# Cross-attention and FFN layer on one core: FFN input tiles transposed by VectorE through DRAM, first weight blocks prepared beside the output projection

## The chip, the cores and the metric

The kernel runs on one core of one Trainium2 chip. The metric is the device time of one execution, in microseconds; lower is better. The runs before the change took 2531.85, 2536.68 and 2537.15 us (median 2536.68).

## The reference

One transformer layer for 16 sequences of 112 tokens (1792 tokens) of width 1024, with a context of 375 vectors for each sequence, all in float32:

```
x = x + attention(layernorm(x), ctx, ctx) @ Wo      # 32 heads, 8 key/value heads
n = layernorm(x)
g = n @ (w1 * w1_scale).T ; u = n @ (w3 * w3_scale).T   # 1024 -> 3584, a scale for each 128x128 block
x = x + (silu(g) * u) @ (w2 * w2_scale).T               # 3584 -> 1024
```

The second layernorm has no weights; its result `n` is the FFN's input. The matrix products want it transposed, with the 1024 features on the partitions.

## The kernel before, in words

The program has four stages, one after the other: `queries`, `attention`, `mixing` (L933), which is the output projection with the residual and the second layernorm, and `ffn` (L1115). Each of the last two is one block of five instruction streams (TensorE, VectorE, ScalarE, GpSimd, and SyncE for the transfers); the streams run in the written order and meet by semaphores. A stage's block ends when all its streams have ended, SyncE's with waits for its last stores. Every product of float32 operands is done as three products of a high and a low part (`split_product`, L84 to L86), so operands are first copied to the high part by ScalarE and the rest is taken by VectorE (`to_lo`, L90).

`mixing` goes over 14 tiles of 128 tokens. For tile t, SyncE loads the attention's output and the rows of x (`load_tile`), ScalarE and VectorE split the attention's output (L1000, L90), TensorE makes two column halves of 512 in two PSUM banks with 48 matmuls, and VectorE runs `residual_norm(t)`: two residual adds (L1042) with the statistics of each half (L1047), the aggregate, GpSimd's power for 1/sqrt (L992), and the normalization (L1058) into `xn`. TensorE then transposes the eight 128x128 blocks of `xn` of the tile before (`transposes(t - 1)`, L1099) after the products of tile t, and ScalarE copies them (`out_x`, L1012) into `xT` for the first seven tiles, or into `xs`, which SyncE stores to `x_scratch`, for the last seven. SyncE also stores the sum to `y_scratch` (L978). In SyncE's order, `load_tile(t + 1)` stands behind the wait for the adds of tile t - 1, in front of the wait for those of tile t.

`ffn` works with Strassen-like sums: a product of a pair of 2x2 blocks is done by seven matmul groups instead of eight. There are 28 first-layer weight blocks (`mi`), w1 and w3 in turn, in two passes over the two halves of the tokens. A weight block is loaded raw (`load_raw`, L168, four transfers of 32 partitions each, by which the quarters of the columns land on the quarters of the partitions), scaled by ScalarE (L1540), transposed by VectorE in blocks of 32x32 (`make_wT`, L1643; with that placement this is the full transpose), summed (`sums`, L1666 to L1671) and split (L1558, L90). The seven inputs `x_source(g, i)` are blocks of `xT` and sums of them (`x_sums`, L1694), split in the same way (L1567, L90). Before its loop the stage has a head: weight block 0, the x sums, all seven splits of x and of weight block 0, and the transposes of weight block 1. TensorE takes product i of block mi when both splits of index i are there; its product i = 5 of block 0 waits also for the first add of results (`add`, L1699), which stands in VectorE's stream behind the head. What comes later (second pass, down projection) is as in the code and is touched by the change in small places only.

Of the kernel before, what the change touches and what calls it, by code (L numbers as in the profile page):

```python
# [21 lines left out]
def build_program(nc, x, ctx, wq, wk, wv, wo, w1, w1_scale, w3, w3_scale, w2, w2_scale, out):  # L22
# [49 lines left out]
    y_scr = nc.dram_tensor("y_scratch", [TOK, D], f32).ap()  # L72
    h_scr = nc.dram_tensor("h_scratch", [7, P, NP, HALF], f32).ap()
# [23 lines left out]
    with top:  # L97
# [34 lines left out]
        raw_loaded = sem("raw_loaded")  # L132
        q_stored = [sem(f"q_stored{c}") for c in range(NG * J)]
# [799 lines left out]
        def mixing(xT):  # L933
            with ExitStack() as st:
# [9 lines left out]
                yb, xn = sb("yb", [P, 2, D]), sb("xn", [P, 2, KT, P])  # L944
                xs = sb("xs", [P, 2, KT, P])
# [7 lines left out]
                t_done, t_out = s_("t_done"), s_("t_out")  # L953
                o_bank, t_bank = bank[0:2], bank[2:4]

                with nc.Block() as block:
                    @block.sync
                    def _(sp):
# [8 lines left out]
                        def store_xT(t):  # L967
                            sp.wait_ge(t_out, 2 * t + 2)
                            cols = slice((t - MT) * P, (t - MT + 1) * P)
                            sp.dma_start(x_scr[:, :, cols], xs[:, t % 2, :, :]  # L970
                                         ).then_inc(xT_stored[t % 2], 16)
# [10 lines left out]
                        store_xT(NT_TOK - 1)  # L982

                        for s in range(2):
                            sp.wait_ge(res_stored[s], 16 * NT_TOK // 2)
                            sp.wait_ge(xT_stored[s], 16 * ((MT + s) // 2))
# [9 lines left out]
                    def _(act):  # L996
# [6 lines left out]
                        def out_x(t):  # L1003

                            if t >= MT:
                                wait(act, xT_stored[t % 2], 16 * ((t - MT) // 2))
                            for kh in range(2):
                                act.wait_ge(t_done, 2 * t + kh + 1)
                                ks = slice(KH * kh, KH * kh + KH)
                                dst = (xT[:, ks, t * P:(t + 1) * P] if t < MT  # L1010
                                       else xs[:, t % 2, ks, :])
                                nc.scalar.activation(dst, t_bank[kh][:, :].rearrange(  # L1012
                                    "p (k q) -> p k q", k=KH), ACT.Copy).then_inc(t_out, 1)
# [6 lines left out]
                        for t in range(1, NT_TOK):  # L1020
                            if t + 1 < NT_TOK:
                                split_attention(t + 1)
                            out_x(t - 1)
                            if t == 4:
                                place_scales(act)
                        out_x(NT_TOK - 1)

                    @block.vector
                    def _(dve):
# [5 lines left out]
                        def residual_norm(t):  # L1035
# [3 lines left out]
                            for n in range(2):  # L1039
                                cols = slice(n * FB, (n + 1) * FB)  # L1040
                                dve.wait_ge(o_done, 2 * t + n + 1)
                                nc.vector.tensor_tensor(yb[:, slot, cols], o_bank[n][:, :],  # L1042
# [13 lines left out]
                            wait(dve, t_done, 2 * (t - 1))  # L1056

                            nc.vector.tensor_scalar(  # L1058
                                xn[:, slot, :, :].rearrange("p b (q j) -> p q b j", q=Q4),
                                yb[:, slot, :].rearrange("p (q b j) -> p q b j", q=Q4, j=BL),  # L1060
                                aggr[:, 0:1], rstd[:], ALU.subtract, ALU.mult
# [53 lines left out]
        def ffn(xT):  # L1115
            with ExitStack() as st:
# [275 lines left out]
                with nc.Block() as block:  # L1392
# [140 lines left out]
                    def _(act):  # L1533
# [63 lines left out]
                        for mi in range(2 * NM):  # L1597
                            P_, nxt = mi // 2, mi + 1 < 2 * NM
                            for i in range(7):
# [11 lines left out]
                                if nxt:  # L1611
                                    split_w(mi + 1, i)
# [220 lines left out]
```

## Time and profile before

| | before |
|---|---|
| runs, us | 2531.85, 2536.68, 2537.15 |
| the profiled execution's own time, us | 2538.41 |
| its span, first to last instruction, us | 2536.6 |
| mean granted TensorE clock | 0.977 of full speed |
| TensorE matmuls busy | 2427.8 us, 96% |
| VectorE busy | 1698.4 us, 67% |
| ScalarE busy | 979.2 us, 39% |
| `mixing`, first split to the last x_scratch store | about 862 to 1041 us |
| `ffn`, from its first ScalarE instruction | 1041.17 us on |

Rows of a timeline give the start in us from the span's start, the duration, the engine (SPq is SyncE's transfer queue; its duration is that of issuing), the line, what is written and read with the size, and in brackets how long the engine was idle before it and what ended that. A busy share is no measure of what a stage's end depends on; the chain of waits and the timeline of the stage are.

### The profile page before, as it was taken

Reading aid. Unit: us, or ns where it says so; the run is one execution under the profiler, and the core shown is the slowest. Engines: PE = TensorE matmul, PEld = TensorE weight load, DVE = VectorE, ACT = ScalarE, POOL = GpSimd, SP = SyncE. Lnnn points to the kernel's source line nnn. Section 1 sums busy time; section 2 is a strip of 40 time slices with the busy share of each in tenths; the row PEclk is TensorE's granted clock in tenths of the full one; section 3 lists DMA queues with packets and bytes.
Section 4 is the critical chain, followed back from the end, with each engine's and each line's share of the span. In section 5 each row is a group of like instructions: output and inputs, shape, how many; then the busy total and the mean of one; then the engine's idle time right before and its main releaser. Section 6 shows DMA issues by size and latency. Waiting matters only on the chain.

```text
span 2536.6 us, 35412 instructions
## 1 busy us (share of the span) xinstructions
PE 2427.8 (96%) x12682; PEld 2071.4 (82%) x12682; DVE 1698.4 (67%) x2639; ACT 979.2 (39%) x1673; POOL 559.2 (22%) x305
## 2 busy tenths in 40 slices
PE   7998999999999799599999998999999999999999
PEld 6997878878875488489999987988988978888887
DVE  6425777777776344688888888888888874445442
ACT  3212445445444321354444444444433443233231
POOL 1000344454455300001111111322333320000000
PEclk9998999999998799799999999999999999999999
DMA  7535555555545335456555564565776687555652
GB/s 226 173 92 138 140 139 139 144 134 142 143 110 131 95 127 170 119 183 184 159 176 156 158 179 134 158 174 190 208 209 176 172 287 234 172 174 160 183 161 86
DMA packets 369146, 408.04 MB, mean 161 GB/s; under 512 B 125824, under 2 KB 324096, under 8 KB 359152
## 3 DMA queue, kind: packets, MB, share of 16 engines
q1 hardware_dynamic: 369008, 406.22, 56.1%
q8 instruction: 85, 1.39, 0.2%
q14 instruction: 53, 0.43, 0.1%
HBM read 252.99 MB, written 152.70 MB: 160 GB/s over the span
## 4 chain that ended last, share of the span: by engine, by line
PE 44%; DVE 8%; DMA 3%; issue 2%; SPq 1%; ACT 1%; DVEq 0%; ACTq 0%
PE bank L84 15%; PE bank L85 14%; PE bank L86 14%; DMA stash<-weight_scratch 3%; DVE g_WL L90 2%; DVE g_XL L90 1%; DVE g_su L1699 1%; DVE xT L1655 1%; SPq L1431 1%; DVE stash L1667 1%; DVE stash L1666 1%; DVE stash L1669 1%; ACT stash L1548 0%; ACT g_WH L1558 0%; DVE stash L1643 0%
## 5 line engine op out<-in xcount | busy, mean ns | idle before, releaser
L84 PE MATMUL bank<-g_XH,g_WH 128*128 128x448 f32 (+1 forms) x2254 | 848.0, 376 | 51.8 <-DVE g_su L1699 24.2
L85 PE MATMUL bank<-g_XL,g_WH 128*128 128x448 f32 (+1 forms) x2254 | 845.0, 375 | 0.0
L86 PE MATMUL bank<-g_XH,g_WL 128*128 128x448 f32 (+1 forms) x2254 | 844.8, 375 | 0.0
L84 PEld LDWEIGHTS bank<-g_XH,g_WH 128*128 128x128 f32 x2254 | 425.2, 189 | 115.8 <-DVE g_WL L90 52.8
L86 PEld LDWEIGHTS bank<-g_XH,g_WL 128*128 128x128 f32 x2254 | 425.2, 189 | 54.1
L85 PEld LDWEIGHTS bank<-g_XL,g_WH 128*128 128x128 f32 x2254 | 425.4, 189 | 53.5
L1558 ACT ACTIVATE g_WH<-stash 128x512 fp32r<-128x512 f32 x392 | 241.7, 627 | 427.6 <-PE bank L86 247.0
L90 DVE TENSOR_TENSOR g_WL<-stash,g_WH 128x512 fp32r<-128x512 f32 (+1 forms) x417 | 336.0, 809 | 77.4 <-ACT g_WH L1558 49.4
L696 DVE TENSOR_REDUCE a_nm<-bank 112x1 f32<-112x375 f32 x512 | 264.9, 531 | 116.9 <-PE bank L831 113.3
L800 ACT ACTIVATE a_pr<-bank 125x448 f32<-125x448 f32 x384 | 204.8, 545 | 208.2 <-PE bank L907 153.7
L649 POOL TENSOR_TENSOR a_prsum<-a_pr 125x1792 f32<-125x1792 f32 x32 | 129.3, 4039 | 365.3 <-ACT a_pr L800 365.3
L1699 DVE TENSOR_TENSOR g_su<-bank,g_su 128x448 f32<-128x448 f32 x280 | 170.8, 610 | 35.6 <-PE bank L86 35.3
L831 PE MATMUL bank<-a_kst,a_qst 96*112 96x376 f32 x512 | 183.2, 367 | 5.8 <-DVE a_nm L696 2.6
L907 PE MATMUL bank<-a_qst,a_kst 98*125 98x448 f32 x384 | 148.3, 391 | 2.8 <-ACT a_pr L800 2.4
L831 PEld LDWEIGHTS bank<-a_kst,a_qst 96*112 96x112 f32 x512 | 91.7, 179 | 69.7 <-DVE a_nm L696 32.6
L1498 POOL TENSOR_TENSOR g_Sh<-stash 128x448 f32<-128x448 f32 x28 | 32.6, 1165 | 492.5 <-DVE stash L1704 492.5
L645 POOL TENSOR_TENSOR a_prsum<-a_prsum,a_pr 125x1792 f32<-125x1792 f32 x32 | 128.7, 4022 | 1.8
L678 DVE RECIPROCAL a_l<-a_l 128x112 f32<-128x112 f32 x128 | 106.6, 839 | 25.8 <-ACT a_l L754 25.8
L84 PE MATMUL bank<-a_w_h,a_cT_h 128*125 128x256 f32 x384 | 111.8, 291 | 0.0
L86 PE MATMUL bank<-a_w_h,a_cT_l 128*125 128x256 f32 x384 | 107.8, 281 | 0.0
L85 PE MATMUL bank<-a_w_l,a_cT_h 128*125 128x256 f32 x384 | 107.7, 280 | 0.0
L1285 ACT ACTIVATE g_WH<-stash 128x1792 fp32r<-128x1792 f32 x25 | 42.6, 1703 | 156.8 <-PE bank L86 146.3
(132 smaller groups left out, 3592.8 us busy)
## 6 DMA issues: line engine op xcount, KB each, us to landing
stash<-in_L_ffn_w SPq DMA_DIRECT2D x168, 256.0 KB, 5.1
weight_scratch<-stash SPq DMA_DIRECT2D x28, 1024.0 KB, 7.7
stash<-weight_scratch SPq DMA_DIRECT2D x28, 1024.0 KB, 7.4
h_scratch<-g_Sh SPq DMA_DIRECT2D x112, 224.0 KB, 3.9
down_scratch<-xT SPq DMA_DIRECT2D x98, 256.0 KB, 3.1
stash<-in_ctx SPq DMA_DIRECT2D x48, 500.0 KB
stash<-h_scratch SPq DMA_DIRECT2D x25, 896.0 KB, 6.7
a_qst<-q_scratch SPq DMA_DIRECT2D x96, 224.0 KB, 4.7
```

Of the source, the lines that this page charges most:

```text
L84: pe.matmul(acc, lh, rh, start=first, stop=False, skip_group_check=onto)
L85: pe.matmul(acc, lh, rl, start=False, stop=False, skip_group_check=onto)
L86: return pe.matmul(acc, ll, rh, start=False, stop=last, skip_group_check=onto)
L90: return nc.vector.tensor_tensor(dst, src, hi.bitcast(f32), ALU.subtract)
L645: pool.tensor_tensor(prsum[:], prsum[:], pr[0:CK, :, 2, :], ALU.add).then_inc(all_added, 1)
L649: pool.tensor_tensor(prsum[:], pr[0:CK, :, 0, :], pr[0:CK, :, 1, :], ALU.add).then_inc(two_added, 1)
L696: nc.vector.tensor_reduce(nm[:, 1 - par, h:h + 1], s_bank[h % 2][0:SQ, 0:SK], AX.X, ALU.max, negate=True).then_inc(max_done, 1)
L800: nc.scalar.activation(pr[0:CK, r, c, :], st_bank[u % 2][0:CK, 0:J * SQ], ACT.Exp, scale=SCALE).then_inc(exp_done, 1)
L831: pe.matmul(s_bank[h % 2][0:SQ, 0:SKP], qst[0:96, 1 - par, g, j * SQ:(j + 1) * SQ], kst[0:96, 1 - par, g, :], start=True, stop=True).then_ ...
L907: pe.matmul(st_bank[u % 2][0:CK, 0:J * SQ], kst[0:98, par, g * R + r, c * CK:(c + 1) * CK], qst[0:98, par, g * R + r, :], start=True, stop ...
L1558: nc.scalar.activation(WH[:, i, :, :], w_source(mi, i), ACT.Copy).then_inc(w_hi, 1)
L1699: nc.vector.tensor_tensor(su[:, slot, :], acc[mi % 2][:, 0:TB], su[:, other, :], ALU.add).then_inc(summed, 1)
```

## The change

The transposes of the layernorm's output leave TensorE. `residual_norm(t)` writes `xn` in plain order, SyncE stores it to a new DRAM tensor `n_scr`, waits until that store has landed, and loads it back with four transfers in the same quarter placement as the raw weights (`load_turn`); VectorE transposes it with two 32x32-block transposes (`turn_tile`, called by `turn`). For the last tile this is done in `ffn`, while block 0 runs. The matmuls of a tile now use one of two pairs of banks, by the tile's parity. SyncE's order in a tile is new, and so is VectorE's, where `turn(t - 1)` stands in front of `residual_norm(t)`. Part of the head of `ffn` (weight block 0 whole, weight block 1 up to its sums, two of the x sums) is spread over tiles 6 to 12 of `mixing` by the class `Ahead`. The semaphores of the down projection's `load_y` are shared by two tiles, with a wait for the tile two before.

```diff
+        def load_turn(sp, dst, t, loaded):
+            cols = n_scr[t * P:(t + 1) * P, :].rearrange("(c i) (q n) -> q i c n", i=BL, q=Q4)
+            for q in range(Q4):
+                sp.dma_start(dst[q * BL:(q + 1) * BL, :, :], cols[q]).then_inc(loaded, 16)
+
+        def turn_tile(src, dst, turned):
+            src = src.rearrange("p c (b j) -> p b c j", j=BL)
+            dst = dst.rearrange("p b (c j) -> p b c j", j=BL)
+            nc.vector.transpose(dst[:, 0:KH], src[:, 0:KH])
+            return nc.vector.transpose(dst[:, KH:KT], src[:, KH:KT]).then_inc(turned, 1)
...
+                        def load_xr(t):
+                            sp.wait_ge(xn_stored[t % 2], 16 * (t // 2 + 1))
+                            wait(sp, turned, t - 1)
+                            load_turn(sp, xr[:, t % 2, :, :], t, xr_loaded[t % 2])
+
                         for t in range(NT_TOK):
-                            if 1 <= t < NT_TOK - 1:
-
-                                sp.wait_ge(y_done, 2 * t)
-                                load_tile(sp, t + 1)
                             sp.wait_ge(y_done, 2 * t + 2)
+                            if t + 2 < NT_TOK:
+                                load_tile(sp, t + 2)
                             sp.dma_start(y_scr[t * P:(t + 1) * P, :], yb[:, t % 2, :]
                                          ).then_inc(res_stored[t % 2], 16)
                             if t > MT:
                                 store_xT(t - 1)
-                        store_xT(NT_TOK - 1)
+                            sp.wait_ge(xn_done, t + 1)
+                            sp.dma_start(n_scr[t * P:(t + 1) * P, :], xn[:, t % 2, :]
+                                         ).then_inc(xn_stored[t % 2], 16)
+                            if t + 1 < NT_TOK:
+                                load_xr(t)
+                            if t == 9:
+                                ahead.load_raw(sp)
...
+                        def turn(t):
+                            dve.wait_ge(xr_loaded[t % 2], 64 * (t // 2 + 1))
+                            if t >= MT:
+                                wait(dve, xT_stored[(t - 1) % 2], 16 * ((t - MT + 1) // 2))
+                            turn_tile(xr[:, t % 2, :, :], xT[:, :, t * P:(t + 1) * P] if t < MT
+                                      else xs[:, :, :], turned)
...
                         for t in range(1, NT_TOK):
                             if t + 1 < NT_TOK:
                                 split_attention(t + 1)
+                            turn(t - 1)
                             residual_norm(t)
+                            ahead.vector(t, turned, w_lo)
...
                         for t in range(1, NT_TOK):
                             products(t)
-                            transposes(t - 1)
-                        transposes(NT_TOK - 1)
...
+                    def scalar(t):
+                        if t == 6:
+                            act_scale_raw(0, 0)
+                            act_scale_raw(0, 1)
+                        for i in W_AT.get(t, ()):
+                            act_split_w(0, i)
+                        if t == 11:
+                            act_scale_raw(1, 0)
+                            act_scale_raw(1, 1)
...
+                    def vector(t, turned, wo_split):
+                        if t == 7:
+                            nc.vector.wait_ge(wo_split, NG * J)
+                            nc.vector.wait_ge(sc_placed, 3 * Q4)
+                            for n in range(4):
+                                dve_make_wT(0, n)
+                        if t == 8:
+                            dve_sums(0)
+                        if t == 9:
+                            nc.vector.wait_ge(turned, MT)
+                            dve_x_sums(0, 0)
+                            dve_x_sums(0, 1)
+                        for i in W_AT.get(t, ()):
+                            dve_split_w(0, i)
+                        if t == 12:
+                            for n in range(4):
+                                dve_make_wT(1, n)
+                            dve_sums(1)
+
+                W_AT = {9: (0, 1), 10: (2, 3), 11: (4, 5), 12: (6,)}
...
                         split_x(0, 0)
-                        split_w(0, 0)
-                        x_sums(0, 1)
-                        x_sums(0, 2)
+                        dve_x_sums(0, 2)
                         split_x(0, 1)
-                        split_w(0, 1)
                         split_x(0, 2)
-                        split_w(0, 2)
-                        x_sums(0, 3)
-                        for n in range(4):
-                            make_wT(1, n)
+                        dve_x_sums(0, 3)
                         for i in range(3, 7):
                             split_x(0, i)
-                            split_w(0, i)
...
+                                if mi == 0 and i == 1:
+                                    dve.wait_ge(last_loaded, 64)
+                                    turn_tile(last_in, last_out, last_turned)
...
                         for mi in range(2 * NM):
                             if mi == 2:
+                                sp.wait_ge(last_turned, 1)
+                                sp.dma_start(x_scr[:, :, HALF - P:HALF], last_out
+                                             ).then_inc(last_stored, 16)
...
                 def load_y(sp, r, t):
+                    if t >= 2:
+                        sp.wait_ge(d_y_loaded[r][t % 2], y_count(r, t - 2))
```

## Rows read from the trace of the kernel before

**Rows 1.** The page: busy shares, and the chain that ended last.

```profile
PE 2427.8 (96%) x12682; PEld 2071.4 (82%) x12682; DVE 1698.4 (67%) x2639; ACT 979.2 (39%) x1673; POOL 559.2 (22%) x305
...
PE 44%; DVE 8%; DMA 3%; issue 2%; SPq 1%; ACT 1%; DVEq 0%; ACTq 0%
```

**Rows 2.** Timeline of TensorE in `mixing`: a tile's products begin, its transposes follow.

```profile
1008.91 0.48 PE L84 MATMUL bank<-m_w_h,m_a_h 128*128 128x512 f32 x1
...
1019.90 1.04 PE L1099 MATMUL bank<-ident,m_xn 128*128 128x128 f32 x8
```

**Rows 3.** Timeline of VectorE: second residual adds of tiles 0, 1, 12 and 13.

```profile
879.85 0.67 DVE L1042 TENSOR_TENSOR m_yb<-bank,stash 128x512 f32<-128x512 f32 x1
...
889.55 0.68 DVE L1042 TENSOR_TENSOR m_yb<-bank,stash 128x512 f32<-128x512 f32 x1
...
890.88 0.67 DVE L1042 TENSOR_TENSOR m_yb<-bank,stash 128x512 f32<-128x512 f32 x1
...
1020.10 0.69 DVE L1042 TENSOR_TENSOR m_yb<-bank,stash 128x512 f32<-128x512 f32 x1 [0.34 <-PE bank L86]
...
1022.62 0.81 DVE L1058 TENSOR_SCALAR m_xn<-m_yb,m_aggr,m_rstd 128x1024 f32<-128x1024 f32 x1 [0.66 <-POOL m_rstd L992]
...
1031.88 0.69 DVE L1042 TENSOR_TENSOR m_yb<-bank,stash 128x512 f32<-128x512 f32 x1 [3.93 <-PE bank L86]
```

**Rows 4.** Timeline of SyncE's queue: transfers that follow tile 2's adds.

```profile
903.02 0.33 SPq L978 DMA_DIRECT2D y_scratch<-m_yb  x1
903.39 0.55 SPq L157 DMA_DIRECT2D stash<-attn_scratch  x1
903.99 0.92 SPq L159 DMA_DIRECT2D stash<-in_x  x1
```

**Rows 5.** Windows (stretch, length, engines, clock, DMA share, GB/s): those three transfers.

```profile
903.50:904.00 0.50, 0.50 (x4) 0.42 (x3) 0.43 (x3) 0.33 (x1) 0.00 (x0) 1.00 0.32 131
904.00:908.50 4.50, 4.50 (x22) 3.72 (x21) 0.97 (x2) 0.28 (x1) 0.55 (x1) 1.00 1.00 325
908.50:909.00 0.50, 0.50 (x4) 0.42 (x3) 0.00 (x0) 0.50 (x1) 0.00 (x0) 1.00 0.24 90
```

**Rows 6.** Windows: the same with an x_scratch store between; that store alone.

```profile
1009.50:1010.00 0.50, 0.50 (x4) 0.42 (x3) 0.45 (x3) 0.41 (x1) 0.00 (x0) 1.00 0.30 123
...
1016.50:1017.00 0.50, 0.50 (x4) 0.42 (x3) 0.00 (x0) 0.50 (x1) 0.00 (x0) 1.00 0.07 25
...
1033.50:1036.50 3.00, 1.09 (x8) 0.86 (x8) 1.02 (x3) 0.47 (x1) 0.55 (x1) 1.00 0.92 319
...
1038.50:1040.00 1.50, 0.00 (x0) 0.00 (x0) 0.00 (x0) 0.00 (x0) 0.00 (x0) 0.50 0.98 290
1040.00:1040.50 0.50, 0.00 (x0) 0.00 (x0) 0.00 (x0) 0.00 (x0) 0.00 (x0) 0.50 0.31 87
```

**Rows 7.** One line of the DMA issues: count, size, median us to landing.

```profile
y_scratch<-m_yb SPq DMA_DIRECT2D x14, 512.0 KB, 3.1
```

**Rows 8.** Window during one raw weight block's load (four transfers of 32 partitions).

```profile
1047.50:1051.00 3.50, 0.00 (x0) 0.00 (x0) 3.50 (x3) 0.00 (x0) 0.00 (x0) 0.50 1.09 198
```

**Rows 9.** Timeline of VectorE and ScalarE: first instructions of `ffn`.

```profile
1041.17 2.56 ACT L1540 ACTIVATE stash<-stash,sc 128x512 f32<-128x512 f32 x4 [4.06 <-PEq L956]
...
1042.54 2.53 DVE L1643 STREAM_TRANSPOSE stash<-stash 128x512 f32<-128x512 f32 x4 [7.32 <-ACT stash L1540]
```

**Rows 10.** Timeline of the head: a split of x, a sum, the first results' add.

```profile
1056.10 1.70 ACT L1567 ACTIVATE g_XH<-stash 128x1792 fp32r<-128x1792 f32 x1 [10.27 <-DVE stash L1694]
...
1057.83 2.03 DVE L90 TENSOR_TENSOR g_XL<-stash,g_XH 128x1792 fp32r<-128x1792 f32 x1 [1.76 <-ACT g_XH L1567]
1059.77 0.68 DVE L90 TENSOR_TENSOR g_WL<-stash,g_WH 128x512 fp32r<-128x512 f32 x1
...
1080.13 0.69 DVE L90 TENSOR_TENSOR g_WL<-stash,g_WH 128x512 fp32r<-128x512 f32 x1
...
1081.49 0.71 PE L84 MATMUL bank<-g_XH,g_WH 128*128 128x448 f32 x1 [6.36 <-DVE g_su L1699]
```

More of the change, by code:

```diff
@@ L930, in _, with mixing @@
                         sums(B - 1, 1)
-        def mixing(xT):
+        def mixing(xT, ahead):
             with ExitStack() as st:
@@ L1092, in products @@
                                 last.then_inc(o_done, 1)
-                        def transposes(t):
-                            pe.wait_ge(xn_done, t + 1)
-                            for kh in range(2):
-                                wait(pe, t_out, 2 * t + kh - 1)
-                                for k in range(KH):
-                                    last = pe.transpose(t_bank[kh][:, k * P:(k + 1) * P],
-                                                        xn[:, t % 2, KH * kh + k, :], ident[:])
-                                last.then_inc(t_done, 1)
                         pe.wait_ge(a_lo, 1)
@@ L1178, in hcols, with act_scale_raw @@
                     return slice(g * TB, (g + 1) * TB)
+                def act_scale_raw(mi, s):
+                    p, m = mi // 2, mi % 2
+                    nc.scalar.wait_ge(raw_loaded, 64 * (mi + 1))
+                    for a in range(2):
+                        part = raw[:, 4 * a:4 * a + 4, s * P:(s + 1) * P]
+                        nc.scalar.activation(part, part, ACT.Copy,
+                                             scale=sc13[:, m, 2 * p + a, s:s + 1]
+                                             ).then_inc(raw_scaled, 1)
@@ new lines, in dve_sums @@
+                def dve_sums(mi):
+                    a11, a12, a21, a22 = [quarter(mi, a, b) for a in range(2) for b in range(2)]
+                    s1, s2, s3, s4 = (S[:, k, :, :] for k in range(4))
+                    if mi < NM:
+                        nc.vector.wait_ge(wT_made, 4 * mi + 4)
+                    else:
+                        nc.vector.wait_ge(wT_loaded[mi % 2], 16 * ((mi - NM) // 2 + 1))
+                    wait(nc.vector, w_lo, 7 * mi)
+                    nc.vector.tensor_tensor(s1, a21, a22, ALU.add).then_inc(S_made, 1)
+                    nc.vector.tensor_tensor(s3, a11, a21, ALU.subtract).then_inc(S_made, 1)
+                    nc.vector.wait_ge(S_made, 4 * mi + 1)
+                    nc.vector.tensor_tensor(s2, s1, a11, ALU.subtract).then_inc(S_made, 1)
+                    nc.vector.wait_ge(S_made, 4 * mi + 3)
+                    nc.vector.tensor_tensor(s4, a12, s2, ALU.subtract).then_inc(S_made, 1)
@@ new lines, in dve_split_w, with dve_x_sums @@
+                def dve_split_w(mi, i):
+                    nc.vector.wait_ge(w_hi, 7 * mi + i + 1)
+                    to_lo(WL[:, i, :, :], w_source(mi, i), WH[:, i, :, :]).then_inc(w_lo, 1)
+                def dve_x_sums(g, n):
+                    b11, b12, b21, b22 = (block_of(s, t) for s in range(2) for t in range(2))
+                    out, left, right = ((t1[:, :, :], b12, b11), (b12, b22, b12),
+                                        (t2(g), b22, t1[:, :, :]), (t2(g), b21, t2(g)))[n]
+                    if n in (1, 2, 3):
+                        nc.vector.wait_ge(T_made, 4 * g + {1: 1, 2: 1, 3: 3}[n])
+                    if g:
+                        nc.vector.wait_ge(x_loaded_, 16)
+                        if n == 2:
+                            nc.vector.wait_ge(wT_made, 4 * NM)
+                    if n == 3:
+                        nc.vector.wait_ge(x_lo, 7 * g + 2)
+                    nc.vector.tensor_tensor(out, left, right, ALU.subtract
+                                            ).then_inc(T_made, 1)
@@ L1245, in load_a, with y_count @@
                                  ).then_inc(d_a_loaded[n % 2], 16)
+                def y_count(r, t):
+                    return sum(32 * len(rows(r, u)) for u in range(t % 2, t + 1, 2))
                 def load_y(sp, r, t):
+                    if t >= 2:
+                        sp.wait_ge(d_y_loaded[r][t % 2], y_count(r, t - 2))
                     for at, n, tok in rows(r, t):
@@ L1728, in _ @@
                                 dve.wait_ge(prod, 7 * mi + i + 1)
-                                if i == 0 and nxt:
-                                    sums(mi + 1)
+                                if i == 0 and nxt and mi:
+                                    dve_sums(mi + 1)
                                 if i == 1:
```

190 lines of the change are left out of this document (72 added, 118 removed).

## The prediction

> **What bounds the kernel now.** I read the page first: TensorE is busy 96% of the span, and the chain that ended last is TensorE's in its largest part [rows 1]. Then the timelines of the stretch that the change touches, engine by engine. In `mixing` the reader is to see a stage paced by TensorE: tile 13's products begin at 1008.91 and its transposes are 1.04 us behind them; VectorE's second residual add waits for matmuls (0.34 and 3.93 us idle before it) [rows 2, 3]. I call the end of that add Y. Y of tile 0 is 879.85 + 0.67 = 880.52, Y of tile 13 is 1032.57: 152.05 us for 13 tiles, 11.70 each [rows 3]. The head of `ffn` is the other thing: its first instruction runs at 1041.17, and product i = 5 of block 0 starts only at 1081.49, after 6.36 us of waiting for VectorE [rows 9, 10]. There VectorE is the bound. So I count three pieces: Y0 to Y13, Y13 to the start of `ffn` (1041.17 - 1032.57 = 8.60), and from there to that product (40.32).
>
> **Tiles of mixing.** Removed: eight transposes per tile on TensorE (1.04) [rows 2] and the copies by ScalarE. By TensorE alone a tile would then take at most 1019.90 - 1008.91 = 11.0 us. But VectorE's new order makes a ring: xn(t), store to DRAM, its landing, load back, its landing, turn(t), and only then the adds of tile t + 1, from which xn(t + 1) comes. Nothing in it overlaps with itself, so its length is the least period of a tile. Step by step from Y(t), for tiles before the first x_scratch store:
>
> SyncE issues at once the attention load, the x load and the y store; they are the three transfers of [rows 4] in another order. Their bytes began 0.8 us after the first issue (903.02 to 903.84, by the share 0.32 of that half microsecond) and ended at 908.62: 4.8 us of transfer [rows 5]. The normalization ends 1022.62 + 0.81 - 1020.79 = 2.64 after Y [rows 3], so the new store is issued at Y + 2.66, while the three are still moving until Y + 0.03 + 0.8 + 4.8 = 5.65. With one more store in between, the busy stretch grew from 4.8 to 6.7 us (1009.85 to 1016.53) at a full share [rows 5, 6]: transfers of this queue add up. I therefore put the new store behind them. It has the shape of the y store: y and x_scratch stores together run at 319 GB/s, 3.3 us for 1.05 MB, the x_scratch store alone at 290 GB/s, 1.8 to 1.9 us, so 1.4 for it [rows 6]. It ends at 7.05. The y store lands 3.1 us after issue [rows 7], of which 0.8 and 1.4 are explained, so completion is 0.9: landed at 7.95. The load back: 0.8, then 0.52 MB in quarters of 32 partitions, which go at 198 GB/s (2.65 us) [rows 8], then 0.9: 4.35, landed at 12.3. The turn: two of the transposes of which four took 2.53, so 1.27 [rows 9]. The adds with everything ready: 889.55 to 891.55, 2.0 [rows 3]. The next Y is at Y + 15.6.
>
> From t = 8 to 11 the x_scratch store (1.9) is ahead of the new one too: 17.5. At t = 12 there is no tile to load: y, x_scratch and new store end at 0.03 + 0.8 + 1.4 + 1.9 + 1.4 = 5.55, and the ring is 5.55 + 0.9 + 4.35 + 3.27 = 14.1. Sum: 8 x 15.6 + 4 x 17.5 + 14.1 = 208.9 us against 152.05: +56.9.
>
> Bounds of the period. Below, if the new store overtakes the queue: 2.66 + 3.1 + 4.35 + 3.27 = 13.4, or 13 x 13.4 = 174 us (+22). Above, if one more transfer's length shows in every ring, because the quarter loads start late or the halves of the queue are not as well filled as now: 1.9 more per tile [rows 6], +82. I take the sum, because the shares of [rows 5, 6] stand at 1.00 while the transfers add up.
>
> The Trainium skill's page "DMA: Bandwidth & Descriptors", section "Anatomy of one DMA", gives about 2.0 us plus bytes over 436 GB/s, for the GpSimd path; 3.2 for the new store, where [rows 7] have 3.1. By it without a queue the period is the lower bound. The same page of the Trainium skill, "Queues, rings and completion order", says that descriptors on each engine are consumed in ring order, which by the lengthening in [rows 6] the trace agrees with; by that the period is the 15.6 to 17.5. The Trainium skill's rule there ("Rules for kernel authors") that a DMA which reads what another wrote must wait for the other's completion speaks against this change: the completion is paid twice in the ring.
>
> **What lies beside the ring.** TensorE has two pairs of banks now: tile t + 2's products wait for Y(t) and for its splits, and are needed only at Y(t + 1) + 13.6; at half clock too (a warm-up would cost some 2 us) they have over 10 us to spare, so TensorE's saved transposes and lower clock cost or give nothing. The work of `Ahead` on VectorE stands between xn(t) at Y + 2.64 and the turn at Y + 12.3; 9.7 us, of which the attention split needs an estimated 1.4 (twice a 512-wide split of 0.68) [rows 10]. The longest are t = 9, two x sums of 2.03 and two splits of 0.68, 5.4 us, and t = 12, 2.53 for transposes, four sums and a split of 0.7, 6.0 us [rows 9, 10]. Hidden, so 0. If the ring's waits were gone, tile 12 would need 6.0 + 1.4 + 1.27 + 2.0 + 2.64 = 13.3 us of VectorE against TensorE's 11.0, and lose 2. The added raw load at t = 9 (1.05 MB at 198 GB/s, 5.3 us) lies behind the load back and delays the next tile by under 1 us. I leave it at 0.
>
> **End of the stage.** After Y13 the new store's bytes end at 5.55, as at t = 12. Before, `ffn` began 1.0 us after the last store's bytes (about 1040.15 to 1041.17) [rows 6, 9]. So 6.55 instead of 8.60: -2.05.
>
> **Head of ffn.** Left on VectorE's path: the high split of x by ScalarE and its handover (1056.10 to 1057.83, 1.73), and then at VectorE split 0, x sum 2; x sum 2 has to end before ScalarE makes the high part of split 1, a second 1.73 plus 0.05; splits 1 and 2, x sum 3, splits 3 to 6. That is two handovers and nine operations at a pitch of 1.94 (1057.83 to 1059.77): 3.5 + 17.5 = 21.0. Then split, add and product start as before (1080.13 to 1081.49, 1.36): 22.35 [rows 10]. Against 40.32: -18.0. The turn of tile 13 stands behind that add; its 1.27 meets product i = 5 in progress, 2.5 to 4.5 us long, so 0, at most 1.3 lost. TensorE's clock may be up at that point instead of down, up to 2 us gained; I take 0.
>
> **Later parts.** SyncE's new x_scratch store at mi = 2 and the wait for it, some 3 to 4 us, stand where its raw loads have waited for VectorE; `load_y` waits for loads issued two tiles before. 0, at most 4.
>
> **The sum.** 2538.4 (the profiled execution) + 56.9 - 2.05 - 18.0 = 2575.2. That execution is 1.7 above the median of the runs, so 2573.5; I say 2574, slower by 1.5%.
>
> **The rivals.** *The ring without a queue*: the new store passes the loads. +22 - 20 = +2, 2539: no change, in which the ring's cost eats the head's gain. For it: the store is issued only 2.6 us behind. Against it: [rows 6]. The point that decides is a period of 11.70 + 20.05/13 = 13.24 us. *TensorE still paces the tiles*: the round trip from xn(t) to the turn ends within what TensorE's 11.0 leaves, 11.0 - 2.64 - 3.27 = 5.1 us. Then 13 x (11.0 - 11.70) = -9.1, and with -20.05 it is 2508, faster. For it: nothing but that transfers could overlap more than now; against it: one landing alone is 3.1 [rows 7] and there are two. *A longer ring*: the four quarter loads begin late or collide with the next tile's loads, 1.9 more per tile, +25: 2599. That the change does not remove the transposes or move the blocks can be excluded from the code.
>
> **Chances.** Forecast 0.73, longer ring 0.09, no queue 0.11, TensorE paces 0.07. The range of 8 in 10 is 2542 to 2602: it holds the forecast with steps of the ring off by 2 us per tile, the longer ring, and leaves out the faster case and most of the unchanged. A difference of 0.2% (5 us) is about what a measurement of this kernel can tell from none. Faster 0.11 (TensorE paces, and the shorter half of the unqueued ring), same 0.05, slower 0.84.
>
> **What would show it.** In the profile after: the second residual adds 15 to 18 us apart, longer from tile 8 on; VectorE idle for many us before the turn's transposes, released by the load from `norm_scratch`; TensorE idle some 5 us in each tile of `mixing`; `ffn` begins about 6.5 us after the last add, and product i = 5 some 22 us after that. The prediction is wrong if the adds are 11 us apart, if TensorE's products release them, or if the new store lands some 3 us after its issue.

## The result, and the profile after

The changed kernel takes 2586.6 us (median of 4 runs, 2583.8 to 2592.9), the kernel before 2536.4 beside it: 1.0206 times as long, 95% interval 1.0189 to 1.0223. Forecast was 2574, 1.5% slower.

The spans of the two profiled executions (2536.6 and 2582.9) part into the pieces of the prediction. Y is again the end of a tile's second residual add. The last piece starts at product i = 5 of block 0 of `ffn`.

| piece, us | before | after | change | predicted |
|---|---|---|---|---|
| up to Y0 | 880.5 | 878.0 | -2.6 | 0 |
| Y0 to Y13 | 152.05 | 220.3 | +68.2 | +56.9 |
| Y13 to the start of `ffn` | 8.60 | 6.5 | -2.1 | -2.05 |
| from there to product i = 5 | 40.32 | 22.36 | -18.0 | -18.0 |
| from there to the end | 1455.1 | 1455.8 | +0.6 | 0 |
| span | 2536.6 | 2582.9 | +46.3 | +36.8 |

The page of the kernel after, its busy shares and the chain that ended last, against [rows 1]:

```profile
PE 2431.6 (94%) x12570; PEld 2072.0 (80%) x12570; DVE 1711.8 (66%) x2667; ACT 966.0 (37%) x1645; POOL 557.8 (22%) x305
...
PE 44%; DVE 5%; DMA 2%; issue 1%; SPq 1%; ACT 0%; POOL 0%; DVEq 0%
```

TensorE is about as busy as before (2431.6 and 2427.8 us) in a longer span, so the added time is idle time. Its 112 transposes are gone, but its granted clock over the tiles fell from 1.00 to 0.86, and its products took longer. The chain of this kernel reaches back only to 1195.66 us, behind the tiles and the head of `ffn`, so its shares say nothing of either. The waits of the kernel after, 875 to 1100 us (total, times, longest), say who waits in `mixing`:

```profile
PE bank L85 <- DVE m_a_l L91: 45.1, 11, 7.3
DVE xT L182 <- DMA m_xr<-norm_scratch: 43.9, 7, 6.6
DVE m_xs L182 <- DMA m_xr<-norm_scratch: 39.8, 6, 9.1
```

VectorE stands 83.7 us, once in each of 13 tiles, for the load back. That it is idle before 12 of the 13 turns for 5.9 to 9.1 us is the ring seen from VectorE (before the last, 2.1). TensorE's 45 us are a consequence: the attention tile of tile t + 2 is loaded only once the adds of tile t are done, and its split follows. From Y0 on VectorE's adds never waited for TensorE (the one such wait, 4.41 us, is at tile 0). One turn of the ring, tile 2 to tile 3, on VectorE (the add that is Y2; the turn of tile 2; the two adds of tile 3), against [rows 3]:

```profile
911.02 0.68 DVE L1055 TENSOR_TENSOR m_yb<-bank,stash 128x512 f32<-128x512 f32 x1
...
924.83 0.71 DVE L182 STREAM_TRANSPOSE xT<-m_xr 128x512 f32<-128x512 f32 x1 [6.28 <-DMA m_xr<-norm_scratch]
...
926.06 0.65 DVE L1055 TENSOR_TENSOR m_yb<-bank,stash 128x512 f32<-128x512 f32 x1
...
927.36 0.67 DVE L1055 TENSOR_TENSOR m_yb<-bank,stash 128x512 f32<-128x512 f32 x1
```

On SyncE's queue, against [rows 4]:

```profile
911.73 0.55 SPq L159 DMA_DIRECT2D stash<-attn_scratch  x1
912.32 0.66 SPq L161 DMA_DIRECT2D stash<-in_x  x1
913.02 0.43 SPq L996 DMA_DIRECT2D y_scratch<-m_yb  x1
914.37 0.32 SPq L1001 DMA_DIRECT2D norm_scratch<-m_xn  x1
920.39 0.80 SPq L176 DMA_DIRECT2D m_xr<-norm_scratch  x2
```

And in windows (stretch, length, the engines, clock, DMA share, GB/s), against [rows 5]:

```profile
911.50:913.00 1.50, 1.50 (x8) 1.24 (x7) 1.25 (x6) 0.00 (x0) 0.05 (x1) 1.00 0.00 0
913.00:913.50 0.50, 0.50 (x4) 0.41 (x3) 0.00 (x0) 0.00 (x0) 0.50 (x1) 1.00 0.47 131
913.50:914.50 1.00, 1.00 (x6) 0.72 (x4) 0.81 (x1) 0.00 (x0) 0.00 (x0) 1.00 0.83 232
914.50:919.50 5.00, 1.16 (x6) 0.75 (x5) 1.22 (x1) 1.06 (x1) 0.00 (x0) 1.00 0.97 346
919.50:920.00 0.50, 0.50 (x3) 0.42 (x2) 0.00 (x0) 0.00 (x0) 0.00 (x0) 0.66 0.35 139
920.00:920.50 0.50, 0.50 (x3) 0.34 (x2) 0.00 (x0) 0.00 (x0) 0.00 (x0) 0.50 0.00 0
```

The reader is to see the ring in these three views. Y2 is 911.70. The new store is issued at Y + 2.67, and four transfers fill the queue until about 919.7. Only then does SyncE get the landing and issue the load back (920.39), and the turn starts at 924.83; Y3 is 928.03, a period of 16.33 us. The DMA issues of the kernel after (count, size, median us to landing) give the same in one line each; [rows 7] had 3.1 for the first:

```profile
y_scratch<-m_yb SPq DMA_DIRECT2D x14, 512.0 KB, 6.3
norm_scratch<-m_xn SPq DMA_DIRECT2D x14, 512.0 KB, 6.2
m_xr<-norm_scratch SPq DMA_DIRECT2D x52, 128.0 KB, 3.0
```

The last piece looks unchanged (+0.6), yet has a hole. The kernel after, timelines of SyncE, ScalarE and TensorE in the first weight blocks of `ffn`:

```profile
1155.82 0.52 SPq L1580 DMA_DIRECT2D x_scratch<-g_Sh  x1
1165.79 0.35 SPq L1586 DMA_DIRECT2D xT<-x_scratch  x1
...
1171.76 6.80 SPq L170 DMA_DIRECT2D stash<-in_L_ffn_w  x4
```
```profile
1187.40 1.34 ACT L1196 ACTIVATE stash<-stash,sc 128x512 f32<-128x512 f32 x2 [9.67 <-DMA stash<-in_L_ffn_w]
```
```profile
1202.92 0.71 PE L85 MATMUL bank<-g_XH,g_WH 128*128 128x448 f32 x1 [6.48 <-DVE g_su L1755]
```

SyncE stores the last x block, stands 10 us for its landing, and issues the next raw weights only at 1171.76, behind eight other transfers issued since 1165.79 (it takes 6.80 us to issue the four, 1.79 at 1136.50). ScalarE waits for them, then VectorE, then TensorE for 6.48 us. What hides this loss in the piece's sum is told under the eighth and tenth experiment.

### The profile page after: what moved, and what is told of

Same layout as the page of the kernel before. It is cut to its first block, busy times and chain, and to the rows that moved or that the text cites. A ratio compares the mean times of both kernels' runs of the same rounds, so it can differ in the third digit from the quotient of the medians.

```text
span 2582.9 us, 35260 instructions
## 1 busy us (share of the span) xinstructions
PE 2431.6 (94%) x12570; PEld 2072.0 (80%) x12570; DVE 1711.8 (66%) x2667; ACT 966.0 (37%) x1645; POOL 557.8 (22%) x305
## 3 DMA queue, kind: packets, MB, share of 16 engines
q1 hardware_dynamic: 379088, 420.90, 56.9%
## 4 chain that ended last, share of the span: by engine, by line
PE 44%; DVE 5%; DMA 2%; issue 1%; SPq 1%; ACT 0%; POOL 0%; DVEq 0%
PE bank L85 15%; PE bank L87 15%; PE bank L86 15%; DMA stash<-weight_scratch 2%; DVE g_WL L91 1%; DVE g_su L1755 1%; DVE g_XL L91 1%; DVE xT L1747 1%; DVE stash L1234 1%; SPq L1559 0%; DVE stash L1233 0%; DVE stash L1236 0%; DVE stash L1760 0%; ACT stash L1671 0%; ACT g_WH L1206 0%
## 5 line engine op out<-in xcount | busy, mean ns | idle before, releaser
L85 PE MATMUL bank<-m_w_h,m_a_h 128*128 128x512 f32 x224 | 98.1, 438 | 54.4 <-DVE m_a_l L91 45.1
```

The lines of the kernel that those rows point to most:

```text
L85: pe.matmul(acc, lh, rh, start=first, stop=False, skip_group_check=onto)
```

## The experiments

Theory: the ring decides, because the turn stands ahead of the next tile's adds, and its length is the queue plus two landings. Rivals: the added traffic alone is the cost (15 MB through one queue); VectorE's added work; TensorE's granted clock (0.86 over 880 to 1098 us). Each kernel is the changed one with the edit shown; ratios are to the kernel before, run beside it (its medians there were 2529.9 to 2532.6).

**1. The turn behind the next normalization.**

```
 for t in range(1, NT_TOK):          # VectorE
-    turn(t - 1)
     residual_norm(t)
     ahead.vector(t, turned, w_lo)
+    turn(t - 1)
```
(and SyncE issues `store_xT(t - 1)` behind the new store)

> VectorE runs the turn of tile t - 1 behind the adds and the normalization of tile t instead of ahead of them (the x_scratch store follows it in SyncE's order); every transfer, wait for a landing and operation is kept. Ring theory (the adds of tile t + 1 wait for store, landing, load, landing, turn of tile t): the ring is cut, tiles up to 7 go at TensorE's 11 us, those after at the 12 to 12.5 us that SyncE's waits need; first to last second add 8 x 11.2 + 5 x 12.5 = 152 us instead of 220; total 2586.6 - 68 + 2 = about 2520. Rival, the transfers' own load or VectorE's added work paces the stage: no change by the order, 2575 to 2590.

Measured: 2523.8 us, 0.9967 (0.9952 to 0.9982), so about 60 us less than the changed kernel with every byte and instruction of it kept. Y0 to Y13 is 153.5, as expected. On VectorE the second add of tile 3 (Y3), its normalization, the turn of tile 2, and the add that is Y4:

```profile
913.84 0.67 DVE L1055 TENSOR_TENSOR m_yb<-bank,stash 128x512 f32<-128x512 f32 x1
...
916.34 0.81 DVE L1070 TENSOR_SCALAR m_xn<-m_yb,m_aggr,m_rstd 128x1024 f32<-128x1024 f32 x1 [0.66 <-POOL m_rstd L1017]
918.61 0.71 DVE L182 STREAM_TRANSPOSE xT<-m_xr 128x512 f32<-128x512 f32 x1 [1.46 <-DMA m_xr<-norm_scratch]
...
924.69 0.67 DVE L1055 TENSOR_TENSOR m_yb<-bank,stash 128x512 f32<-128x512 f32 x1
```

The period is 10.85 us with the same turn in it, and the wait for the load back has shrunk to 1.46. Its waits, 875 to 1050 us:

```profile
DVE xT L182 <- DMA m_xr<-norm_scratch: 11.0, 6, 3.9
...
PE bank L85 <- DVE m_a_l L91: 8.3, 5, 5.3
```

The ring theory holds: the position of the turn costs what was measured, and neither VectorE's work nor the traffic does. The granted clock over the tiles is 0.98 here, so this run doesn't test the clock by itself; in the changed kernel no add waited for TensorE from Y0 on, and the clock is off the path for that reason. One period is still long, 16.4 from Y10 to Y11, two tiles behind the raw load; in experiment 9, where that load is issued two tiles earlier, the long one (15.4) is from Y8 to Y9.

**2. The same traffic, without the wait for it.** The turn reads `xn` in place.

```
 def turn(t):
-    dve.wait_ge(xr_loaded[t % 2], 64 * (t // 2 + 1))
+    dve.wait_ge(xn_done, t + 1)
...
-    turn_tile(xr[:, t % 2, :, :], ...
+    turn_tile(xn[:, t % 2, :].rearrange("p (c n) -> p c n", n=DQ), ...
```

> The turn reads the normalized tile in place, without the way through DRAM, so the quarters of the columns are not exchanged between partitions and the FFN gets wrongly placed inputs; the store to DRAM and the load back are still issued and waited for by SyncE, at their places, but VectorE does not wait for them. Ring theory: only the wait cost time; adds 11 us apart up to tile 8, at most 12.5 behind; about 2516. Rival, the traffic of 1 MB more per tile costs it by contention: more than half of the 50 us stays, 2560 or more.

Measured: 2528.0 us, 0.9984 (0.9973 to 0.9994); Y0 to Y13 162.1. So of the 68 us some 10 are left (152.05 to 162.1), nearly all of it in the periods from t = 8 to 11 (13.9, 14.0, 16.8, 13.5 us): there SyncE issues the new store at 1003.65, say, and the load back behind its landing at 1014.05, and all later loads stand behind that wait. These 10 are the traffic and SyncE's own wait together, and the traffic's part is small: the first experiment has the same bytes and needs 153.5. The other 58 are VectorE's wait.

**3. The y and x_scratch stores behind the load back.**

```
+    load_xr(t)                       # SyncE, order within a tile
     sp.dma_start(y_scr[...], yb[...])
     if t > MT: store_xT(t - 1)
-    load_xr(t)
```

> The ring is kept, but the y store and the x_scratch store are issued behind the load back instead of ahead of the new store. Queue theory (transfers of the queue go one after the other): landing of the new store comes 1.5 us earlier up to tile 8 and 3 us earlier at tiles 8 to 11, 8 x 1.5 + 4 x 3 = 24 us less, about 2563. Rival, the ring is made of fixed latencies and the queue ahead does not matter: no change, 2587.

Measured: 2580.7 us, 1.0193 (1.0172 to 1.0214): a miss, 2563 was expected. From tile 1 up to tile 8 the step is there: 14.5 to 15.8 us per tile instead of 16.3 to 16.8, 1.5 less on the mean as expected, with the load back issued at Y + 6.8 to 7.3 (tile 0 keeps 16.85). From tile 8 on the periods are 17 to 18, because of a wait I had left out. VectorE in this kernel:

```profile
1014.72 0.71 DVE L182 STREAM_TRANSPOSE m_xs<-m_xr 128x512 f32<-128x512 f32 x1 [8.29 <-DMA x_scratch<-m_xs]
```

The turn now waits for the store of the single `m_xs` buffer, which had been sent to the end of the queue. In all Y0 to Y13 gained 12.7 us; the end of the stage lost 2.6 and the last piece 6.7 (below). The y store ahead of the new store is a part of the ring, 1.5 us of it per tile; from tile 8 on, moving it and the x_scratch store only moves the wait.

**4. The moved blocks alone.** Transposes by TensorE and copies by ScalarE as before, no trip through DRAM; two bank pairs and `Ahead` as in the changed kernel.

```
-    turn(t - 1)                      # VectorE
+    transposes(t - 1)                # TensorE, into bank[4:6]
+    out_x(t - 1)                     # ScalarE
```

> One part of the change alone: the first weight blocks and two x sums spread over the tiles, the banks in pairs, but the transposes by TensorE with ScalarE's copies as before, nothing through DRAM. The head part is worth -18 us by my sum and the tiles stay at 11.7 us, so about 2518 (2536.4 - 18). Rival, the work moved into the tiles delays VectorE's adds or collides with the attention split: tiles longer, 2530 or more.

Measured: 2517.3 us, 0.9944 (0.9926 to 0.9963). Y0 to Y13 is 151.5 with a pitch of 11.78, TensorE's, and the head 22.37. The blocks prepared ahead cost these tiles nothing, and they are the gain of the change at the head of `ffn`; only the 2.1 us at the end of the stage are not theirs.

**5. The load back issued a tile later.** Over the first experiment, SyncE issues `load_xr(t - 1)` at the head of tile t.

```
     for t in range(NT_TOK):          # SyncE
+        if 0 < t < NT_TOK - 1:
+            load_xr(t - 1)
         sp.wait_ge(y_done, 2 * t + 2)
...
-        if t + 1 < NT_TOK: load_xr(t)
+        if t == NT_TOK - 2: load_xr(t)
```

> As in the run with the turn behind the normalization, but SyncE never waits for the new store's landing: it issues the load back of tile t - 1 at the head of tile t, when that store has long landed, and VectorE turns tile t - 1 behind the normalization of tile t; for tile 12 alone the order of the changed kernel is kept. Ring theory with the sum of transfers as the next bound: tiles before 8 at TensorE's 10.9 us, those from 8 on at the 11.7 us of their six transfers; first to last add 147 us; 6 us below the first cut, tail 6.5 instead of 10.3: about 10 us faster than that run. Rival, the transfers collide (load back ahead of the attention load delays the splits that TensorE waits for): no faster than it.

Measured: 2531.9 us, 0.9999 (0.9984 to 1.0015): a miss, 10 us less than the first was expected. Y0 to Y13 is 162.4, 9 us more than the first. The other tiles gain nothing (Y0 to Y12 143.5, there 142.1), as the rival had it, and most of the loss is one tile: Y12 to Y13 takes 18.94 (11.41 there), because there the turn stands ahead of the adds again, as in the changed kernel. VectorE before Y13:

```profile
1033.45 0.70 DVE L182 STREAM_TRANSPOSE m_xs<-m_xr 128x512 f32<-128x512 f32 x1
...
1040.97 0.71 DVE L182 STREAM_TRANSPOSE m_xs<-m_xr 128x512 f32<-128x512 f32 x1 [6.22 <-DMA m_xr<-norm_scratch]
```

**6. The turn through DRAM alone,** with no block prepared during `mixing`.

```
 def vector(t, turned, w_lo):         # and scalar(t), load_raw(sp)
-    if t == 7: ... dve_make_wT(0, n)
-    if t == 8: dve_sums(0)
...
+    pass
```

> The other part of the change alone: the transposes go through DRAM and VectorE as in the changed kernel, but nothing of the FFN's head is moved into the tiles. The ring sets the tiles with or without that work, so the head comes back in full, +18 us, and the tiles keep their 16 to 19 us (220 us from first to last add, some 3 less without the raw load at tile 9): the changed kernel + 15 to 18. Rival, the moved work lengthens the ring: the tiles get clearly shorter without it and less than 10 us are lost.

Measured: 2610.1 us, 1.0304 (1.0277 to 1.0332), by the ratios 25 more than the changed kernel, where 15 to 18 were expected. Its Y0 to Y13 is 218.4, 2 less than with the moved blocks; the tenth experiment, the changed kernel again, has 223.5, so executions of one kernel differ by more than that. TensorE's product i = 5:

```profile
1145.03 0.71 PE L85 MATMUL bank<-g_XH,g_WH 128*128 128x448 f32 x1 [6.35 <-DVE g_su L1742]
```

That is 40.3 us after the start of `ffn`: the 18 of the head are back in full. The other 7 are in the last piece (1462.8 for 1455.8).

**7. One landing instead of two.** The load back reads as many bytes from the input x and waits for no store.

```
-    sp.wait_ge(xn_stored[t % 2], 16 * (t // 2 + 1))
-    load_turn(sp, xr[...], t, xr_loaded[t % 2])
+    load_turn(sp, xr[...], t, xr_loaded[t % 2], x.rearrange("b q n -> (b q) n"))
```

> The load back takes the same amount in the same four quarters from the kernel's input x instead of the normalized tile, and is issued right behind the new store without waiting for its landing; so the FFN gets untreated inputs. The ring loses the gap between the store's last byte and the first byte loaded, 1.3 us at tile 2, and keeps both transfers: from 16.4 to about 14.9 up to tile 8 and 16.6 behind it, first to last add about 200 instead of 220, the changed kernel - 20. Rival, one landing is worth a whole latency of 3 us: 13.4 per tile, - 40.

Measured: 2563.1 us, 1.0115 (1.0087 to 1.0142). SyncE and VectorE in tile 3:

```profile
911.65 0.33 SPq L1001 DMA_DIRECT2D norm_scratch<-m_xn  x1
912.02 1.04 SPq L176 DMA_DIRECT2D m_xr<-in_x  x1
```
```profile
920.21 0.71 DVE L182 STREAM_TRANSPOSE xT<-m_xr 128x512 f32<-128x512 f32 x1 [4.11 <-DMA m_xr<-in_x]
```

The load back is issued at once, and still lands only at the end of the queue: the periods are 14.3 to 14.6 (t = 1 to 7), 2.1 less than after, where the forecast of the ring gives 1.7 less (0.8 and 0.9); from t = 8 to 11, 15.8 to 16.4. Y0 to Y13 is 193.2 where about 200 were expected; that the time met its forecast (20 below the changed kernel) is in part luck, since the last piece took 7.8 us more (1463.6). So the first landing by itself is worth 2 us per tile, and the larger part of the ring is the queue. The Trainium skill's page "DMA: Bandwidth & Descriptors", section "Rules for kernel authors", wants a transfer that reads what another wrote to wait for that one's completion; this run is what the rule costs here.

**8. The last x block's store earlier.** In `ffn` SyncE stores it as soon as the block is turned, ahead of the raw weight loads.

```
+    sp.wait_ge(last_turned, 1)
+    sp.dma_start(x_scr[:, :, HALF - P:HALF], last_out).then_inc(last_stored, 16)
     ...                              # the raw loads of mi = 1, 2
-        sp.wait_ge(last_turned, 1)
-        sp.dma_start(x_scr[:, :, HALF - P:HALF], last_out).then_inc(last_stored, 16)
```

> The changed kernel, with one transfer moved: SyncE stores the last tile's transposed block to x_scratch before block 0's raw-weight loads in its order (right behind the second weight store), not at mi = 2 behind them. In the changed kernel SyncE stands 10 us between that store and the load of xT, the next raw load comes late, ScalarE waits 9.7 us for it and TensorE has a hole of 6.5 us. If that wait is the cause, the hole goes: the changed kernel - 6 us, with TensorE's wait and ScalarE's wait for the raw load gone from the profile. Rival, the hole comes from GpSimd's sums beside VectorE's sums (both 1.6 us instead of 0.7 to 1.2 there): it stays.

**10. The changed kernel again,** run beside it.

> The changed kernel itself on the same chip as the two others, as their measure: 50 us above before, ratio 1.02.

Measured: 2585.0 us, 1.0194 (1.0171 to 1.0217), against 2587.5, 1.0208 (1.0190 to 1.0226) for the unchanged order: by time no difference that can be told. In the profile the hole is gone. SyncE and ScalarE's waits (1130 to 1210 us) in the eighth experiment:

```profile
1130.97 0.52 SPq L1577 DMA_DIRECT2D x_scratch<-g_Sh  x1
...
1158.73 0.34 SPq L1586 DMA_DIRECT2D xT<-x_scratch  x1
...
1172.77 4.42 SPq L170 DMA_DIRECT2D stash<-in_L_ffn_w  x4
```
```profile
ACT stash L1196 <- DMA stash<-in_L_ffn_w: 5.3, 2, 3.8
```

The store has 28 us to land instead of 10, and the largest step from one of TensorE's products to the next there is 1.0 us, where it was 6.9 and, in the tenth, 5.8. What took the gain away is the pitch of the products. A stretch of 100 us, all of it at the full granted clock and with TensorE busy throughout: the kernel after, the kernel before, the eighth experiment.

```profile
1250.00:1350.00 100.00, 100.00 (x495) 92.67 (x494) 87.34 (x130) 48.83 (x83) 17.93 (x12) 1.00 0.58 170
```
```profile
1200.00:1300.00 100.00, 100.00 (x485) 90.83 (x484) 85.63 (x126) 48.06 (x83) 17.91 (x12) 1.00 0.57 168
```
```profile
1250.00:1350.00 100.00, 100.00 (x485) 90.83 (x484) 86.96 (x129) 48.44 (x83) 17.92 (x12) 1.00 0.56 164
```

495 products against 485 in the same time: from start to start 0.2027 us against 0.2067. Sorting the profiled executions by the largest pause at the place of the hole and by the pitch behind it, with the last piece of the span in us (from product i = 5):

| | 0.2067 each | 0.2027 each |
|---|---|---|
| no pause over 1.1 us there | before 1455.1; exp. 4, 8, 9, 11, 12: 1451.7 to 1455.4 | none |
| a pause of 5.7 to 6.9 us there | exp. 3, 6, 7: 1462.5 to 1463.6 | after, exp. 1, 2, 5, 10: 1454.8 to 1457.4 |

So the hole costs 7 to 9 us where nothing repays it (1462.5 to 1463.6 against 1454.5 to 1455.4 in before and experiments 8 and 9), and in five of eight executions with a hole the products behind it ran at the shorter pitch for some 1700 of them (1700 x 0.004 = 6.8 us). That also accounts for the 6.7 and 7 us that experiments 3 and 6 were off by in their last piece. A pause doesn't by itself make the pitch the shorter one: in experiments 3, 6 and 7 the products ahead of the hole ran at 0.2027 and those behind it at 0.2067, in 5 and 10 it was the other way round, and in the eighth the pitch grew at a pause of 1.0 us:

```profile
1150.00:1190.00 40.00, 40.00 (x199) 37.07 (x199) 32.59 (x50) 18.10 (x32) 5.98 (x4) 1.00 0.73 238
1210.00:1250.00 40.00, 40.00 (x195) 36.32 (x194) 34.14 (x52) 17.91 (x31) 5.97 (x4) 1.00 0.67 185
```

So the pitch can change either way where TensorE pauses. What decides which it becomes, these runs don't settle.

**9. Experiments 1 and 8 together, and the raw load at tile 7.**

```
-    if t == 9: ahead.load_raw(sp)
+    if t == 7: ahead.load_raw(sp)
```

> Turn behind the normalization, with the early store of the last block, and the raw weight load moved from tile 9 to tile 7, ahead of the tiles that store to x_scratch. Against the run with the turn behind alone (7.6 us under before): -6 for the hole in the FFN, -3 to -5 for the 16.4 us tile 10 that the raw load made long; 16 to 18 us under before, about as fast as the kernel with only the blocks moved ahead. If the queue's sum of transfers holds the tiles anyway, only the 6.

Measured: 2520.0 us, 0.9940 (0.9921 to 0.9959); Y0 to Y13 151.5, and no hole. With three places of its order mended, the change gets to where the moved blocks alone are, and not beyond.

**11. Half by half.** Tiles 0 to 6 are turned through DRAM behind the next normalization, as in the first experiment; 7 to 13 by TensorE and ScalarE.

```
+    if t < MT:                       # SyncE
+        sp.dma_start(n_scr[...], xn[...]).then_inc(xn_stored[t % 2], 16)
+        load_xr(t)
...
+    if t > MT: out_x(t - 1)          # ScalarE, TensorE likewise
```

> The blocks moved ahead, tiles 0 to 6 transposed by VectorE through DRAM with the turn behind the next normalization, tiles 7 to 13 by TensorE. Up to tile 7 the queue carries no x_scratch stores, so tiles go at 10.8 to 11.3 us instead of 11.8; the rest as with the blocks alone, tail included: 7 x 0.7 = 5 us under the kernel with the blocks alone, 2512 if that has 2517. Rival, the five transfers of a tile delay the attention splits that TensorE waits for, as in the piped version: no faster.

**12. The moved blocks alone, again,** run beside it.

> The kernel with the blocks alone, again, on the same chip as the mixed one: 14 us under before, ratio 0.994.

Measured: 2513.5 us, 0.9929 (0.9905 to 0.9953), and 2515.7 us, 0.9931 (0.9907 to 0.9954). In the profile the tiles are 5.4 us shorter (146.1 for 151.5: periods of 10.4 to 11.6 up to tile 8, then 11.78 as by TensorE); in the time the 2 us between them can't be told from nothing. Both beat the kernel before, by 0.7%.

## Why the prediction was right, and where it was off

**The ring.** Right, and shown by experiments 1 and 2: store, landing, load back, landing, turn and adds follow one another, and TensorE and VectorE's other work have room beside them. The signs named in advance came: adds 16 to 19 us apart and longer from tile 8 on, VectorE idle for 6 to 9 us before each turn but the last, TensorE idle in most tiles. Of the rivals, a ring without a queue is excluded (the new store landed 6.0 us behind its issue, not 3), and so is TensorE as the pace (no add waited for it from Y0 on). *A longer ring* named 1.9 us more per tile, +25 in all; the tiles took 11.4 more than forecast, nearly half of that, by the terms that follow.

**The landing of the new store** is the term that was mis-sized. Forecast were 0.8 + 4.8 + 1.4 + 0.9 us from the first issue, landed at Y + 7.95. In tile 3, by the same arithmetic on the windows above: bytes begin, by the share, 1.5 us after the first issue (913.50 - 0.47 x 0.50 = 913.27, for 911.73), are done at 919.50 + 0.35 x 0.50 = 919.68, so 6.4 for the predicted 6.2, and SyncE goes on 0.7 later (920.39). That is Y + 8.69, +0.74, and all of it from the start: the 0.8 of [rows 5] was that of a queue whose first transfer is the y store; here it is the attention load. At t = 12 of the same kernel, where the y store is first again, no byte moves up to 1085.50 and the share is 0.70 from there to 1085.60, 0.8 us behind the issue at 1084.72. For t = 0 to 7 the load back was issued at Y + 8.7 to 9.3, and the mean period was 16.57 for 15.6, +7.8 us in eight tiles. That the transfers of one queue add up, the choice on which the forecast rested against its cheapest rival, held: the new store, issued 2.67 behind Y, landed 6.0 us later. The Trainium skill's page "DMA: Bandwidth & Descriptors", section "Queues, rings and completion order", has descriptors consumed in ring order; with these 6.0 us the trace agrees.

**The load back, turn and adds** were right: 4.44 (4.35 predicted), 1.23 (1.27) and 1.97 (2.0) in that tile.

**The periods from t = 8 to 11**: 17.90, 18.99, 17.89, 19.38 for the predicted 17.5 each, +4.2 in all. Two of them are as the forecast plus part of the same late start. The raw load at t = 9 costs "under 1 us", as said: 18.99 against 18.33 where experiment 6 leaves it out. At t = 11 the 1.7 above the value there (17.70) was not foreseen: the load back took 5.5 us from issue to turn, 1 more than elsewhere. It did so in experiments 8 and 10 too (5.6 and 5.2), and not in 6 (4.4), so it seems to come with the moved blocks; by what way isn't settled. The period at t = 12, 13.56 for 14.1, gave back 0.5. Sum: 7.8 + 4.2 - 0.5 = 11.4 of the 68.2.

**End of the stage** -2.1 for -2.05 and **head of `ffn`** 22.36 for 22.35: right to the tenth, and the head is confirmed both ways, by experiment 4 (its gain alone) and 6 (its loss alone).

**Work beside the ring at 0**: right within what executions differ by (218.4 without the moved blocks, 220.3 to 223.5 with them). TensorE's lower clock did stay off the path: no add waited for it from Y0 on.

**Later parts at 0, at most 4**: this step failed, though the piece's sum (+0.6) doesn't show it. I priced the wait for the new x_scratch store by itself and said that the raw loads have time. They had not: store, landing (10 us) and a load that then stands behind eight others delay the next weights, and TensorE stands 6.5 us. In this execution the products behind the hole ran at the shorter pitch, which gave as much back, so that the piece's sum came out right by luck; in three of the experiments it did not, and the piece took 7 to 9 us more. A step moved past a queue's other work must be priced by what stands behind its wait.

Together the profiled execution was 2584.7 instead of 2575.2: +11.4 in the tiles, -2.6 before Y0 (over all the profiled executions Y0 lies between 878.0 and 881.8), +0.6 at the end.

## What to carry to other kernels

A transpose through DRAM is two landings behind all that the queue holds: here 10.5 us from the new store's issue to the turn (914.37 to 924.83), where the transposes themselves take 1.2. It is nearly free if the consumer stands one tile further back in its engine's order (experiment 1), and costs the whole of it per tile if it stands ahead of the work from which the next round trip starts. So look for a ring: does the instruction that waits for the landing precede, on its engine, the one that produces the next data to be sent? And test the parts of a change apart: here, by the ratios, one part gave 14 to 17 us (experiments 4 and 12) and the other took 77 (experiment 6, in which the hole costs 7 to 8 of them).

## What the runs showed of the hardware that I had not expected

- Two pitches of the same product at the full granted clock, 0.2027 and 0.2067 us for one of 128x448, each steady over hundreds of products, and changing either way at pauses of 1.0 to 6.9 us. Over 1700 products it is worth 6.8 us. Its cause is open.
- The start of the first transfer is not one number: 0.8 us after the first issue with the y store ahead [rows 5], 1.5 (by the share) with the attention load ahead; from the last byte to SyncE going on it is 0.7 there. The Trainium skill's page "DMA: Bandwidth & Descriptors", section "Anatomy of one DMA", puts most of a fixed 2.0 us into completion, for the GpSimd path; no run here uses that path. On SyncE's queue in tile 2 the larger share lies ahead of the first byte, and for this queue the measurement decides.
- SyncE itself can be held in issuing: four quarter loads that take 1.8 us to issue elsewhere took 6.80 and 4.42 above, and the new store, 0.32 us in tile 2, took 3.73 at 1003.65 in the second experiment, behind twelve transfers issued in the 6.4 us before it. That a full queue holds it is my reading; no run varies it alone.
